# Five chunks prepared first, experts behind ten batches in 39 blocks, maxima three and then four units ahead

## The reference, cut to what matters

```python
xn = layernorm(x)                                 # x: 16 batches x 256 tokens x 128
q = (xn @ w_q.T).reshape(16, 256, 16, 8)          # 16 heads of 8
k, v = xn @ w_k.T, xn @ w_v.T                     # one key/value head of 8, shared
attn = softmax(einsum('bshd,btd->bhst', q, k) * scale)
s = einsum('bhst,btd->bshd', attn, v).reshape(16, 256, 128) @ w_out.T

t = (xn * rsqrt(mean(xn * xn) + 1e-5) * norm_scale).reshape(4096, 128)
w = top-2 softmax gates over 8 experts from t @ gate_w + gate_b
y = sum over e of w[:, e] * (swiglu(t @ w1[e] + b1[e]) @ w2[e] + b2[e])   # inner 256
out = x + s * silu(xn + y)
```

## Time and profile before

| | us |
|---|---|
| three runs | 504.22, 516.02, 513.49 |
| median | 513.49 |
| the profiled execution | 505.16 |
| its span | 503.2 |
| 0 to 44.6 us | preparation of nine chunks |
| 44.6 to 75.08 us | maxima of the first four units, up to the first exponential |
| 75.08 to 217.82 us | exponentials of units 0 to 15 |
| 222.90 to 347.40 us | experts |
| 347.40 to 503.20 us | units 16 to 31 and the end |

### The profile page before, as it was taken

How to read it: one execution, slowest core, us unless ns; L and a number is a source line. 1 busy time by engine, 2 the same in 40 slices (tenths; PEclk the granted TensorE clock), 3 DMA queues, 4 the chain that set the end, 5 groups by cost and what they waited for, 6 DMA issues and landing times.

```text
span 503.2 us, 7796 instructions
## 1 busy us (share of the span) xinstructions
PE 397.6 (79%) x2380; PEld 243.5 (48%) x2380; DVE 292.2 (58%) x558; ACT 277.7 (55%) x616; POOL 262.9 (52%) x320
## 2 busy tenths in 40 slices
PE   2685567893995899858999999999158979679894
PEld 1564333341442445337999898986014434234221
DVE  5634988694773767716666666665218667358101
ACT  2247174562672767636666666666217667257673
POOL 3779314220377777701777766767201666366730
PEclk9999565786997989979999999999659898789798
DMA  6211021745152222254666656751711233143100
GB/s 180 77 49 34 0 65 49 285 193 167 45 159 105 87 92 95 91 143 108 165 195 174 174 174 178 193 167 47 226 59 49 89 102 91 64 119 89 34 11 21
DMA packets 48493, 55.92 MB, mean 111 GB/s; under 512 B 11715, under 2 KB 36291, under 8 KB 48326
## 3 DMA queue, kind: packets, MB, share of 16 engines
q1 hardware_dynamic: 43270, 45.84, 30.9%
q0 software_dynamic: 4608, 9.51, 5.4%
q10 hardware_dynamic: 576, 0.08, 0.1%
HBM read 34.86 MB, written 20.08 MB: 109 GB/s over the span
## 4 chain that ended last, share of the span: by engine, by line
PE 44%; DMA 16%; issue 12%; POOL 11%; ACT 6%; DVE 6%; SPq 4%; ACTq 0%; POOLq 0%; DVEq 0%
PE ps L908 14%; DMA qs<-q_dram 14%; PE ps L931 7%; PE ps L795 7%; PE ps L781 5%; PE ps L766 4%; POOL xn_all L413 3%; ACT probs L633 2%; DVE neg L1203 2%; POOL xn_all L487 2%; POOL th L493 2%; PE ps L917 2%; POOL xn_all L482 2%; POOL rows L507 2%; PE ps L744 1%
## 5 line engine op out<-in xcount | busy, mean ns | idle before, releaser
L1203 DVE TENSOR_REDUCE neg<-ps 128x4 f32<-128x1024 f32 x128 | 154.2, 1215 | 95.4 <-PE ps L781 95.3
L633 ACT ACTIVATE probs<-ps 128x512 f32<-128x512 f32 x256 | 141.0, 596 | 88.6 <-PE ps L766 85.4
L781 PE MATMUL ps<-k_stack,qs 72*128 72x256 bf16 x512 | 88.1, 302 | 62.0 <-DMA qs<-q_dram 45.9
L474 POOL DMA_INDIRECT y_dram<-early,xs x80 | 83.9, 1049 | 55.1 <-issue 29.8
L766 PE MATMUL ps<-qs,k_stack 75*128 75x512 bf16 x256 | 95.3, 409 | 6.3 <-ACT probs L633 4.9
L781 PEld LDWEIGHTS ps<-k_stack,qs 72*128 72x128 bf16 x512 | 51.9, 106 | 91.8 <-DMA qs<-q_dram 50.0
L454 POOL DMA_INDIRECT sorted_dram<-rows,pos_i x64 | 61.5, 961 | 44.8 <-DVE eid_i L1149 25.6
L908 PE MATMUL ps<-early,w_st 128*128 128x256 f32 x320 | 77.6, 386 | 2.6 <-ACT early L687 2.4
L795 PE MATMUL ps<-probs,v_all 128*32 128x512 f32 x512 | 77.6, 734 | 0.9 <-ACT probs L633 0.9
L1267 DVE TENSOR_SCALAR early<-ps,b_st 128x256 f32<-128x256 f32 x80 | 35.0, 480 | 49.8 <-PE ps L908 49.8
L908 PEld LDWEIGHTS ps<-early,w_st 128*128 128x128 f32 x320 | 58.8, 194 | 10.4 <-issue 2.8
(11 more groups left out here) (146 smaller groups left out, 399.0 us busy)
## 6 DMA issues: line engine op xcount, KB each, us to landing
w_st<-in_w SPq DMA_DIRECT2D x40, 256.0 KB
qs<-q_dram SPq DMA_DIRECT2D x32, 288.0 KB
sorted_dram<-s_b SPq DMA_DIRECT2D x2, 2600.0 KB, 11.2
xs<-sorted_dram SPq DMA_DIRECT2D x40, 130.0 KB, 3.0
early<-y_dram SPq DMA_DIRECT2D x16, 256.0 KB, 3.9
q_dram<-early SPq DMA_DIRECT2D x16, 192.0 KB, 4.0
out<-rows SPq DMA_DIRECT2D x16, 128.0 KB, 2.3
xn_all<-in_x SPq DMA_DIRECT2D x3, 512.0 KB, 8.4
```

The lines of the kernel that those rows point to most:

```text
L474: gp.indirect_dma_start(out=y_dram, out_offset=bass.IndirectOffsetOnAxis(ap=at[:, t, :], axis=0), in_=ys[:, r, t, :], in_offset=None).then ...
L633: sc.activation(probs[:, u % 2, k, :], ps[:, bank, :], ACT.Exp).then_inc(m["exp_ok"], 1)
L781: last = te.matmul(ps[:, 3 + 2 * (n % 2) + i // 2, (i % 2) * S:(i % 2 + 1) * S], qs[0:KROWS, u % QS, at:at + P], k_stack[0:KROWS, b * S:(b ...
L1203: ve.tensor_reduce(neg[:, b % 2, st, h:h + 4], ps[:, 3 + 2 * (n % 2):5 + 2 * (n % 2), :].rearrange("p a (e t) -> p (a e) t", e=2), AX, ALU ...
```

## The change

Nine things change together.

1. Five chunks are prepared before the first maxima. The other four are prepared inside the attention: their statistics in step w=2, normalised in w=4 and 5, turned and multiplied in w=5 and 6. A step now has two numbers, w for the unit whose maxima it takes and u = `unit_of(w)` for its exponentials.
2. The exponentials follow by three units (w = u+3) up to unit 8; step w=12 has no exponentials; from unit 9 on they follow by four.
3. The tokens of chunks 2 to 8 are normalised on ACT, not on POOL. `xT`, `q`, `kv` and the first keys go through the ring of three banks. The second chunk's queries are split on POOL.
4. `qs` has eight slots, and SP loads the queries of unit u+7. Chunks 2 to 4 are written and units 4 to 7 loaded before the steps begin.
5. Padding goes out in ten transfers, one per step from w=2 to 11. Routing moves to w=7 to 11. ACT fills the rows for the scatter four tiles a step from w=6 to 13.
6. Experts come behind unit 19, in 39 blocks.
7. x is read again in eight transfers during the experts.
8. Nine slots `yb` for expert results. The gate becomes one DVE instruction (th + 1) * f. `s` has a slot for each batch.
9. tanh of batch i comes at step 22 + 9i/16 (before 18 + 3i/4).

```diff
-AHEAD = 4
-QS = 6
+QS = 8
+SWITCH = 12
-BLOCKS = TOPK * TOKENS // ROWS + E
+BLOCKS = TOPK * TOKENS // ROWS + E - 1
-YB = 3
+YB = 9
-EXPERTS_AT = 16
-KEYS_AFTER = 4
+EXPERTS_AT = 20
+LATE = 5
+KEYS_AT, LATE_AT, LATE_KEYS_AT, ROUTE_AT, RANK_AT = 3, 5, 7, 7, 8
-    return EXPERTS_AT + 2 + (3 * i) // 4
+    return EXPERTS_AT + 2 + (9 * i) // 16
+def unit_of(w):
+    if w <= 2 or w == SWITCH:
+        return -1
+    return w - 3 if w < SWITCH else w - 4
+def late_chunks(w):
+    return (LATE + 2 * (w - LATE_AT), LATE + 2 * (w - LATE_AT) + 1) if w in (LATE_AT, LATE_AT + 1) else ()
...
             # SP
-                sp.dma_start(sorted_dram.rearrange("(a p t) c -> p a (t c)", p=P, t=PAD_TILES)[:, half * h:half * h + half, :],
-                             replicated(pad_row[:, :, :].rearrange("p t c -> p (t c)"), half, 1)).then_inc(m["pad_in"], 16)
+                sp.dma_start(sorted_dram.rearrange("(a p t) c -> p a (t c)", p=P, t=PAD_TILES)[:, h, :],
+                             pad_row[:, :, :].rearrange("p t c -> p (t c)")).then_inc(m["pad_in"], 16)
+            def attend(u, w):
+                if 1 <= u and u + 7 < UNITS:
+                    load_q(u + 7)
+                if u == EXPERTS_AT + 1:
+                    for r in range(Y_SLOTS):
+                        sp.wait_ge(y_out[r], 32 * len(range(r, BLOCKS, Y_SLOTS)))
+                for i in range(B):
+                    if EXPERTS_AT + max(1, i // 2) == u:
                         load_y(i)
...
+                if 8 <= w < 12:
+                    write_q(w - 3)
+                if w % 2 == 0 and w <= UNITS:
+                    load_m(w // 2 - 1)
+                if 2 <= w < 12:
+                    fill_pads(w - 2)
...
             # POOL
+            for i in range(B):
+                add_first(i)
+                if i >= 4:
+                    gated(i - 4)
+                add_second(i)
+                if i >= 4:
+                    add_x(i - 4)
...
             # ACT
+            def norm(i):
+                a, n = CHUNKS[i]
+                act.wait_ge(m["nb_ok"], min(i, LATE) - 1)
+                for t in range(a, a + n):
+                    sc.activation(xn_all[:, t, :], xn_all[:, t, :], ACT.Identity, bias=lnb[:, 8, t:t + 1],
+                                  scale=lnb[:, 0, t:t + 1]).then_inc(m["xp_ok"], 1)
...
+                exps(u, 3, 4)
+                if late:
+                    evac_xT(late[0])
+                exps(u, 4, 5)
+                if late:
+                    evac_chunk(late[0])
+                if w % 2 == 0 and w <= UNITS:
+                    evac_mT(w // 2 - 1)
+                for i in late_chunks(w + 1):
+                    norm(i)
...
                 exps(u, 7, 8)
+                if w == KEYS_AT:
+                    late_roots()
+                if 6 <= w < 14:
+                    for t in range(4 * (w - 6), 4 * (w - 6) + 4):
+                        fill_row(t)
...
             # PE
                 scores_exp(u, 3)
-                scores_max(u + AHEAD, 2)
+                if w == 2:
+                    turn_m(0)
+                scores_max(w, 2)
+                if late:
+                    turn_chunk(late[0])
                 scores_exp(u, 4)
+                if late:
+                    chunk(late[0])
+                if w % 2 == 0 and 2 < w <= UNITS:
+                    turn_m(w // 2 - 1)
...
             # DVE
+            def gate(i):
+                f = xn_all[:, 2 * i:2 * i + 2, :].rearrange("p t d -> p (t d)")
+                dve.wait_ge(m["th_ok"], i + 1)
+                ve.scalar_tensor_tensor(f, th[:, i % 3, :], 1.0, f, ALU.add, ALU.mult).then_inc(m["g_ok"], 1)
...
+                    if w == 2:
+                        statistics(LATE + r)
+                    if w == ROUTE_AT and r == 0:
+                        key_rows(2)
+                    if w == ROUTE_AT and r >= 1 or w == ROUTE_AT + 1 and r < 2:
+                        route(0, 3)
+                    if ROUTE_AT + 1 < w <= ROUTE_AT + 4:
+                        route(1, 3)
```

More of the change, by code:

```diff
@@ L385, in _ @@
             load_q(3)
+            for i in range(2, LATE):
+                write_q(i)
+                if i == 2:
+                    for u in range(4, 8):
+                        load_q(u)
             sequence(attend, expert)
@@ L752, in _, with turn_chunk @@
[L752 to L754 removed]
+            def turn_chunk(i):
+                a, n = CHUNKS[i]
+                bank = ring(("xT", i))
+                if i < 2:
+                    pe.wait_ge(m["xn_ok"], a + n)
+                else:
+                    pe.wait_ge(m["xp_ok"], a + n - 4)
+                for t in range(n):
+                    last = te.transpose(ps[:, bank, t * P:(t + 1) * P], xn_all[:, a + t, :], ident[:, :])
+                last.then_inc(m["xT_ps"], 1)
@@ new lines, in chunk @@
+            def chunk(i):
+                n = CHUNKS[i][1]
+                pe.wait_ge(m["xT_sb"], i + 1)
+                if i == 0:
+                    pe.wait_ge(m["wp_in"], 16 * N_WP)
+                    pe.wait_ge(m["w24_ok"], 1)
+                bank = ring(("q", i))
+                te.matmul(ps[:, bank, 0:n * P], wq_sb[:, :], xnT[:, i % 2, 0:n * P], start=True, stop=True
+                          ).then_inc(m["q_ps"], 1)
+                bank = ring(("kv", i))
+                for t in range(n):
+                    last = te.matmul(ps[:, bank, t * 24:(t + 1) * 24], xnT[:, i % 2, t * P:(t + 1) * P],
+                                     w24_sb[:, :], start=True, stop=True)
+                last.then_inc(m["kv_ps"], 1)
```

497 lines of the change are left out of this document (247 added, 250 removed).

## The result

| | median | runs | ratio to the kernel before | 95% interval |
|---|---|---|---|---|
| before | 509.15 us | 504.22 to 516.02 | | |
| changed | 467.81 us | 463.54 to 469.86 | 0.926 | 0.915 to 0.937 |

The ratio is that of the means of the fast runs, and two runs of the kernel before, 513.49 and 516.02 us, were slow and are left out of it. The median is 15.8 us above the 452 that was predicted and inside the range. The profiled execution took 463.54 us, with a span of 461.8.

What follows compares the result with a forecast made beforehand. PE's work was put at 6.7 us a unit, 215 for 32 units, the rest waiting. Experts start at 235, end at 356.6; 3.4 and 90.4 behind them give a span of 450.4, time 452 us, range 436 to 476.

Steps and rivals of the forecast that it cites:

- first exponential: Ahead of the experts, during step w=3: the first exponential runs at about 50 us, against 75 before.
- w=3: Step after the first maxima: four reductions, keys of twelve tiles, some 1.5 for turning and copying; 11 us, to 63.
- w=7 to routing done: Steps w=7 to the middle of w=11: DVE bounds with reductions, 43 routing steps and keys; 44 us, to 148.
- scatters with landing: Between routing and experts: scatters take 80.7 us as before, 148 to 229, and about 2 to land.
- first expert copy: Experts' start: scatter and attention paths both give 235 within 2 us, 12 later than before but behind 20 units.
- Rival B: SP's in-order list keeps part of the query waits; if half of 45.9 us stay, 475 us; chance 9%.
- Steps at nothing: Padding in tenths, later query writes and `s` in 16 slots cost nothing, covered by 20 us of lead.
- That removal is the main gain: PE's query waits, 45.9 us, vanish because loads come three steps, 20 us, ahead; behind the experts, because `qs` is full.
- A: Every unit-loading step: transfer pace, not lead, bounds, with padding pieces at 8.4 us; 546 us in all; chance 4%.
- C: Steps w=4 to 8: PE and ACT wait in turn, routing ends at 160; 464 to 470 us; chance 13%.
- D: Experts: x's pieces ahead of weights in SP's list cost 0.5 us a block, +20, 472 us; chance 4%.
- E: Steps preparing late chunks take only DVE's time, 12 us less; 440 us, inside the forecast's range, which has 70% with it.

Runs made afterwards that it cites:

- the better version: Changed kernel with first maxima transfer issued by ACT, padding two a step, unit u+6's queries loaded in step u, scatter rows six tiles a step: 457.69 us, ratio 0.900.
- all of SP's list as before: Changed kernel with six query slots, unit u+5 loaded in step u, three result slots, result waits and 2 MB of x ahead of next queries: 490.28 us, ratio 0.965.

## Why the prediction was right, and where it was not

The direction, the range and most terms held. What was off is mainly two terms that it left out, both ahead of the experts. For the largest single gain it named one of two conditions; that the change also undid the other, and that the first pair therefore came out as forecast, is in part luck.

| step | predicted | measured |
|---|---|---|
| first maxima | 30 | 32.2 |
| end of w=2 | 52 | 54.0 |
| first exponential | 50 | 60.8 |
| w=3 | 11 | 16.5 |
| w=4 | 11.7 | 11.4 |
| w=5 and 6 | 29 | 30.4 |
| w=7 to routing done | 44, to 148 | 45.7, to 158.0 |
| scatters with landing | 83, to 231 | 83, to 245.7 |
| first expert copy | 235 | 248.7 |
| experts | 121.6 | 122.0 |
| behind them | 93.8 | 91.1 |
| span | 450.4 | 461.8 |

*The step that failed is the first exponential, in "w=3".* The prediction let it come "in here, at about 50". The order of SP's list, shown ahead of the prediction, has the DMAs that stand before the first maxima, but the prediction priced none of them. The exponential came 10.8 us later than that. DVE stood 7.64 us for PE meanwhile. So w=3 took 16.5 us for the 11 of the sum, and all that follows is later by these 5.5. Mending it alone gave back 7.5 at the first exponential and 4.6 at the experts; in the better version it comes at 51.10. Rival B had named the place ("three units of lead in the first phase leave the maxima's own transfer half a step") but looked for it in every step. The later ones cost 1.34 and 1.61 us.

*The second missing term is the padding.* "Steps at nothing (padding in tenths ...)" were said to be covered by the lead of 20 us. A query's lead does nothing for POOL, which waits for the last padding: 4.5 us, gone when it was sent earlier. The better version mends both, and it also loads queries later and fills rows for the scatter earlier. Its routing ends 7.8 us earlier and its scatters start 3.6 us closer behind it: 11.4 of the 13.7 us by which the experts started late. It reached 237.6 where the prediction had 235, and 455.7 where it had 450.4.

*"That removal is the main gain" was right of the waits and half right of their cause.* The waits for queries did go. The longest, 16.3 us, had two conditions. SP's and PE's rows of the kernel before show the first:

```profile
335.91 0.50 SPq L320 DMA_DIRECT2D b_st<-b_col  x1
354.17 1.43 SPq L298 DMA_DIRECT2D early<-y_dram  x3
355.81 0.82 SPq L355 DMA_DIRECT2D rows<-in_x  x1
356.73 6.90 SPq L281 DMA_DIRECT2D qs<-q_dram  x1
```
```profile
370.85 1.03 PE L781 MATMUL ps<-k_stack,qs 72*128 72x256 bf16 x4 [16.33 <-DMA qs<-q_dram]
```

SP issued nothing from 336.4 to 354.17, where it waited for the experts' last results; then came three loads of results and the 2 MB, and only then the load that PE waited for, whose issue took 6.90 us. The second condition is the lead of one unit, which left no time for that. The prediction named what stood ahead ("behind 2 MB of x and three `y` loads") and gave the credit to full slots. It did not name SP's wait.

With the load kept ahead of the waits, a lead of one unit, x in one transfer, or six slots with the short lead leave the pair at 14.1, 16.7 and 14.4 us. With the load behind the waits and the short lead together it takes 28.8 and 32.7. The load moved ahead, in the kernel before, brings it to 22.5. The one case left, the load behind the waits but with three units of lead, was not run. An estimate from the traces: in the changed kernel SP also issues no DMA from 360.8 to 376.23, at no cost. There the load behind the waits would be that of unit 27, whose maxima PE starts at 390.2. SP is past its waits by 378.17, and the 16.7 us from there to PE's release before (354.17 to 370.85) give 394.9: a wait of some 5 us, not 16. So full slots alone would probably have done most of it, and no run shows how the order and the lead share it. Both together are worth 19.5 us in the first pair, about half of the whole gain.

*The other half is explained in part.* The seven other pairs behind the experts took 112.0 us before. The changed kernel with sixteen units behind its experts does the same seven in 93.0, so it isn't the number of units; and with all of SP's list as before the pairs stay short. Of the 19.0 us between them, 7.6 are two waits for queries (2.46 and 5.17), and a wait costs more than its length. Stretches of the kernel before, ahead of the wait of 5.17 us and behind it (columns as in the earlier trace rows):

```profile
418.07:424.70 6.63, 6.39 (x49) 3.36 (x48) 5.24 (x6) 4.80 (x11) 4.38 (x7) 1.00 0.28 77
426.09:432.10 6.01, 0.90 (x5) 0.19 (x2) 1.43 (x3) 2.26 (x6) 4.85 (x7) 0.94 0.46 137
432.16:438.40 6.24, 6.24 (x27) 2.00 (x28) 2.75 (x5) 1.08 (x2) 0.00 (x0) 0.52 0.13 51
```

PE is idle for five of the six us in the second. In the third it is busy throughout at a granted clock of 0.52, the level of 1.2 GHz, and does 27 matmuls where the first had 49 in the same time. The second to fourth of the seven pairs, 55.3 us, hold 44.6 us of PE's work, which takes 38.7 in three clean pairs at full clock: 5.9 more. With the waits, that is 13.5 of the 19.0. The other 5.5 stay open. What let the two waits arise is in neither the slots nor the order around the experts, since the last kernel with both as before has no such wait there. Left are the four instructions for the gate on POOL, of which one on DVE remains, and the stores that SP waits for ahead of later loads. Neither was tried.

*The rivals.* A: no sign of it. Units ahead of the experts take 6.45 us with a DMA share of 0.31. Its price for a padding piece, 8.4 us, was 5.4 in the median. C: steps 5 and 6 took 30.4 together (16.8 and 13.6), not over 17 each. Its size of the routing's end (160 for 158.0 measured) came nearly true, by another mechanism. D: 122.0 us with x riding along, so no. E: the mixed steps took what was said. One sign of being wrong did come: the experts waited on `xs`, because the scatters end at 243.3 and not by 235. The routing chain is the bound there, but only by the 3.4 us from the attention's end (242.3) to the scatters' landing.

*The rules.* The table load ahead of the first exponential starts 1.43 us behind ACT's copy in the first run with the transfer on ACT's queue, and 1.37 of that is the issue of the DMA; in the changed kernel it starts at once. The two loads that the change adds start at 69.85 and 71.50, where the instruction before each ends at 69.84 and 71.48. The drain of 1380 ns that the Trainium skill, "ScalarE: Activation LUTs", "What ACT_TABLE_LOAD costs", adds to each load shows at none of these. The padding moved 520 KB in 5.4 us in the median where it had moved 2600 KB in 11.2, per byte 2.4 times as slow. The rule of the Trainium skill, "DMA: Bandwidth & Descriptors", "Measured (HBM→SBUF, 128 partitions, SWDGE, issued from GpSimd)", to batch to 1 MiB or more, is for loads; these writes go the same way. But the rate did not set the time. The last piece was issued at 153.64, 4.3 us ahead of the routing's end, and landed 8.0 us behind its issue, 2.6 more than the median.

## What to carry to other kernels

Read the DMA issuer's list as the path of an engine: look in the trace for the stretch in which it issues nothing, what wait it stands in, and which load that others want next is behind it. A load that is ready to go belongs ahead of a wait that isn't about it, or needs enough lead to sit the wait out. And price each issue ahead of the first short transfer that a stage starts with, or give that transfer another engine's queue.

## What the runs showed of the hardware

- On two chips nearly nothing but POOL made way during 64 indirect DMAs back to back: 96 matmuls for 525 in the same 80 us, and none of the seven packets of the instruction queues (one, in the kernel before with a line moved) until they were done. On the others there was none of this. Whether the missing instructions are the cause was not tried.
- The issue of four DMAs of 192 KB took 12.9 us of SP's time with four loads of 288 KB issued just ahead of them, up to 6.96 for one, and 5.1 with two. Behind three loads of 256 KB and one of 2 MB the issue of one load took 6.90.
- After a wait of 5.17 us PE ran 6.2 us at a granted clock of 0.52, the level of 1.2 GHz, with 27 matmuls where it had done 49 in about the same time.
